# First phase of a fused decoder layer: queue order, value rows and gate chunks resequenced

## The reference, cut to what matters

```
x = x + attention(layernorm(x))      # 16 heads of 32, one shared K and V head, RoPE,
                                     # K, V squeezed to 8 and grown again, then
                                     # K = quant_dequant_8bit(K), V the same: min and max over ALL sequences
                                     # windows of 128 tokens every 64, sigmoid scores / their sum, blended
x = x + wkv(w, u, layernorm(x), ctx) # a decaying scan over tokens
x = x + ffn(layernorm(x))            # h = silu(q(x) @ tern(Wg)) * (q(x) @ tern(Wu)), rms norm, q(h) @ tern(Wd)
                                     # tern(W) = clip(round(W / mean|W|), -1, 1) * mean|W|
```

## Time and profile before

| | us |
|---|---|
| median of 3 timed runs (1096.98 to 1099.55) | 1097.28 |
| profiled execution, device time | 1100.16 |
| profiled execution, span of the trace | 1098.8 |
| busy: TensorE / VectorE / ScalarE / GpSimd | 878.8 / 844.1 / 706.2 / 435.7 |
| first scores of sequence 0 start | 102.00 |

### The profile page before, as it was taken

How to read it: one execution, slowest core, us unless ns; L and a number is a source line. 1 busy time by engine, 2 the same in 40 slices (tenths; PEclk the granted TensorE clock), 3 DMA queues, 4 the chain that set the end, 5 groups by cost and what they waited for, 6 DMA issues and landing times.

```text
span 1098.8 us, 22051 instructions
## 1 busy us (share of the span) xinstructions
PE 878.8 (80%) x8388; PEld 516.9 (47%) x8388; DVE 844.1 (77%) x1630; ACT 706.2 (64%) x1179; POOL 435.7 (40%) x494
## 2 busy tenths in 40 slices
PE   5883656678888888888888888989898888886665
PEld 2342545445454555555545555555455555553222
DVE  4744477887888888888887888888877888876953
ACT  0114737276868686868777777777786868684633
POOL 2100113236263635353535453535454444444522
PEclk9986776869999999999999999999999999997878
DMA  8876424020515151515142524242424343212022
GB/s 328 314 231 246 151 100 148 19 85 10 103 59 103 55 107 54 107 51 99 63 95 67 84 78 84 78 84 79 84 78 72 91 67 95 68 59 40 28 59 67
DMA packets 125754, 106.90 MB, mean 97 GB/s; under 512 B 99312, under 2 KB 101088, under 8 KB 124496
## 3 DMA queue, kind: packets, MB, share of 16 engines
q1 hardware_dynamic: 119344, 101.47, 35.6%
q0 software_dynamic: 624, 2.59, 0.7%
q10 hardware_dynamic: 5680, 1.42, 0.6%
HBM read 65.62 MB, written 10.49 MB: 69 GB/s over the span
## 4 chain that ended last, share of the span: by engine, by line
ACT 30%; PE 26%; DVE 20%; issue 15%; SPq 5%; DMA 2%; POOL 2%; DVEq 0%; ACTq 0%; POOLq 0%
PE bank L508 9%; ACT arena L734 6%; PE bank L607 5%; PE bank L527 4%; ACT L786 3%; ACT sums L741 3%; DVE junk L1160 3%; PE bank L597 3%; ACT sums L746 2%; ACT junk L786 2%; ACT junk L791 2%; DVE amax L1126 2%; DVE fs L1169 2%; ACT L757 2%; ACT L734 2%
## 5 line engine op out<-in xcount | busy, mean ns | idle before, releaser
L597 PE MATMUL bank<-w_up_gate,qT 128*128 128x512 bf16 x1024 | 244.9, 389 | 40.4 <-ACT junk L786 20.6
L1364 POOL TENSOR_TENSOR work<-junk,lnw 128x512 f32<-128x512 f32 x128 | 188.3, 1491 | 126.0 <-DVE junk L1160 111.7
L1347 POOL TENSOR_TENSOR sums<-sums,blend 128x448 f32<-128x448 f32 x64 | 73.6, 1170 | 274.2 <-ACT sums L746 274.2
L597 PEld LDWEIGHTS bank<-w_up_gate,qT 128*128 128x128 bf16 x1024 | 97.2, 100 | 155.8 <-ACT junk L786 26.3
L508 PE MATMUL bank<-wide,wq_sb 128*128 128x256 f32 x512 | 120.8, 397 | 34.8 <-DVE rows L1061 30.8
L607 PE MATMUL bank<-w_down,work 128*128 128x512 bf16 x512 | 132.0, 408 | 19.8 <-ACT junk L786 10.5
L508 PEld LDWEIGHTS bank<-wide,wq_sb 128*128 128x128 f32 x512 | 100.6, 199 | 61.2 <-issue 46.9
L734 ACT ACTIVATE arena<-bank 128x384 f32<-128x384 f32 x256 | 104.9, 497 | 36.0 <-PE bank L527 35.8
L527 PE MATMUL bank<-wide,k_win 32*128 32x128 f32 x1536 | 69.7, 317 | 72.9 <-ACT arena L734 54.2
L786 ACT ACTIVATE junk<-bank,deq 128x512 f32<-128x512 f32 x128 | 86.3, 686 | 54.0 <-PE bank L597 52.2
L559 PE MATMUL bank<-wo_sb,wide 128*128 128x512 f32 x256 | 115.8, 607 | 2.6 <-DVE wide L1054 2.6
(11 more groups left out here) (150 smaller groups left out, 1536.9 us busy)
## 6 DMA issues: line engine op xcount, KB each, us to landing
sums<-in_xT SPq DMA_DIRECT2D x8, 1024.0 KB, 11.2
wide<-in_xT SPq DMA_DIRECT2D x16, 512.0 KB, 3.8
rows<-in_x SPq DMA_DIRECT2D x16, 512.0 KB, 4.9
ctx_T<-in_ctxT SPq DMA_DIRECT2D x16, 512.0 KB, 3.7
wide<-wide SPq DMA_DIRECT2D x64, 128.0 KB, 2.0
out<-rows SPq DMA_DIRECT2D x32, 256.0 KB, 2.1
kv_b<-k_raw SPq DMA_DIRECT2D x16, 384.0 KB
work<-in_wgT SPq DMA_DIRECT2D x4, 1024.0 KB, 16.4
```

What stands on the lines that cost most here:

```text
L597: last = te.matmul(bank[4 + k % 4][:, :], qT[:, c, t * P:(t + 1) * P], w_up_gate[:, m, c, cols], start=c == 0, stop=c == NC - 1)
L1364: ge.tensor_tensor(hid_w[:, t, cols], hid[:, n % 2, :], lnw[:, cols], op=ALU.mult).then_inc(z_set.sem, 1)
```

## The change

On SyncE: `wkvT` and `low_rank` lead the queue, in place of ScalarE's; `wkvT` is laid out so that each partition reads one piece of 1536 B. In each pair the columns come before the rows. The wait for the small weights goes. `wq` and `xT` of sequence 0 are issued within pair 5. Gate chunks 2 and 3 are issued after the swaps of sequence 0.

```
+        sy.dma_start(wkv_sb.rearrange("p c n -> p (c n)"), a["wkvT"]).then_inc(first_loads.sem, 16)
+        sy.dma_start(low_rank, a["low_rank"]).then_inc(first_loads.sem, 16)
         for j in range(PAIRS):
+            load_columns(j)
             load_x(j)
-            load_columns(j)
-            if j == 0:
-                sy.wait_ge(first_loads.sem, first_loads.at(0))
             if j >= 3:
                 store_trig(j - 3)
-        sy.dma_start(wq_sb[:, :, :], ...)
-        load_queries(0)
+            if j == 5:
+                sy.dma_start(wq_sb[:, :, :], ...)
+                load_queries(0)
         load_keys(0)
         load_weights(GATE, 0)
+        store_trig(5)
         load_weights(GATE, 1)
-        store_trig(5)
-        load_weights(GATE, 2)
-        load_weights(GATE, 3)
         store_trig(6)
...
                 turn_queries(b, 1)
+            if i == 0:
+                load_weights(GATE, 2)
+            if i == 0:
+                load_weights(GATE, 3)
```

```
             se.copy(raw[j % 4], grown).then_inc(key_raw.sem, 1)
-            se.dma_start(v_scratch[2 * j:2 * j + 2].rearrange("u (t p) e -> p (u t) e", p=P), v_raw[j % 4])...
+            new = bank[TOK_BANK[j % 2]][:, 0:4 * 2 * HD].rearrange("p (u t g e) -> p g u t e", u=2, t=NT, g=2)[:, 1]
+            se.copy(v_rows[j % 4][:, :, 0:NW:2, :], new).then_inc(val_rows.sem, 1)
+            se.copy(v_rows[j % 4][0:BLK, :, 1, :], new[BLK:P, :, 0, :]).then_inc(val_rows.sem, 1)
+            se.copy(v_rows[j % 4][BLK:P, :, 1, :], new[0:BLK, :, 1, :]).then_inc(val_rows.sem, 1)
+            se.wait_ge(val_rows.sem, val_rows.at(j))
+            se.dma_start(v_scratch[j], v_rows[j % 4])...
...
-            windows = bass.AP(v_scratch.tensor, v_scratch[b].offset, [[HD, P], [BLK * HD, NW], [1, HD]])
-            sy.dma_start(v_q, windows).then_inc(kv_loaded.sem, 16)
+            sy.dma_start(v_q, v_scratch[pair, :, b % 2]).then_inc(kv_loaded.sem, 16)
```

More of the change, by code:

```diff
@@ L158, in build @@
     raw = [small(P, 2 * 2 * NT * HD).rearrange("p (g n e) -> p g n e", g=2, n=2 * NT) for k in range(4)]
-    v_raw = [raw[k][:, 1] for k in range(4)]
+    v_rows = [home[:, n * 2 * NW * HD:(n + 1) * 2 * NW * HD].rearrange("p (u k e) -> p u k e", u=2, k=NW) for home in
+              (q_tok[:, :, :].rearrange("p t d -> p (t d)").bitcast(fp32), qT[:, :, :].rearrange("p c s -> p (c s)").bitcast(fp32))
+              for n in both]
     wkv_sb = small(P, NC * 3 * HD).rearrange("p (c n) -> p c n", c=NC)
@@ L212, in build @@
     key_grown, key_raw, key_ext = event("key_grown", 2), event("key_raw", 2), event("key_ext", 2)
+    val_rows = event("val_rows", 3)
     w_summed, w_round, w_bound, w_tern = [
@@ L462, in keys_grow @@
                 te.wait_ge(key_raw.sem, key_raw.at(j - 1))
+            if j >= 2:
+                te.wait_ge(val_rows.sem, val_rows.at(j - 2))
             te.matmul(bank[6][0:HD, :], grown_by[:, 0:HD], roped.rearrange("p u s -> p (u s)"), start=True,
@@ L494, in tensor_program @@
                 keys_grow(j - 1)
-            if j == PAIRS - 1:
+            if j == PAIRS - 2:
                 te.wait_ge(wq_loaded.sem, wq_loaded.at(0))
@@ L502, in queries @@
                 te.wait_ge(wq_centred.sem, wq_centred.at(0))
-                te.wait_ge(key_raw.sem, key_raw.at(PAIRS - 2))
+                te.wait_ge(val_rows.sem, val_rows.at(PAIRS - 2))
             if b:
@@ L670, in scalar_program @@
     def scalar_program(se):
-        se.dma_start(wkv_sb, a["wkvT"].rearrange("(c p) n -> p c n", p=P)).then_inc(first_loads.sem, 16)
-        se.dma_start(low_rank, a["low_rank"]).then_inc(first_loads.sem, 16)
         for dst, src in ((ident[:, :], "ident"), (rope_kv, "rope_kv")):
@@ L795, in scalar_program @@
         sum_weights(GATE, 1)
-        sum_weights(GATE, 2)
         for i in range(B + 3):
@@ L818, in scalar_program @@
                 probs(b, 0)
+            if i == 0:
+                sum_weights(GATE, 2)
             if do_f:
@@ L822, in scalar_program @@
                 probs(b, 1)
+            if i == 0:
+                sum_weights(GATE, 3)
+            if do_b:
                 probs(b, 2)
@@ L1000, in vector_program @@
                 keys_rope(j)
+            if j == PAIRS - 1:
+                queries_centre()
             if j:
@@ L1282, in vector_program @@
                 round_weights(DOWN, 3)
-            if i == 0:
-                round_weights(GATE, 1)
             if do_w:
@@ L1292, in vector_program @@
                 round_weights(UP, 1)
+            if i == 0:
+                weight_mean(GATE)
+            if i == 0:
+                round_weights(GATE, 0)
+            if i == 0:
+                round_weights(GATE, 1)
             if do_f:
@@ L1484 @@
         "wqT": g["L0_attn_wq"].reshape(H, HD, D)[:, PAIRED].reshape(D, D).T, "woT": g["L0_attn_wo"].T,
-        "wkvT": np.concatenate([wk[PAIRED], wk[PAIRED], g["L0_attn_wv"]]).T,
+        "wkvT": np.concatenate([wk[PAIRED], wk[PAIRED], g["L0_attn_wv"]]).T.reshape(NC, P, 3 * HD).transpose(
+            1, 0, 2).reshape(P, NC * 3 * HD),
         "low_rank": np.concatenate([squeeze.T, grow_k, grow_v], 1),
@@ L1497 @@
     k_scratch = nc.dram_tensor("k_raw", (B, HD, 3 * S), fp32).ap()
-    v_scratch = nc.dram_tensor("v_raw", (B, S, HD), fp32).ap()
+    v_scratch = nc.dram_tensor("v_raw", (B // 2, P, 2, NW, HD), fp32).ap()
     build(nc, a, out, k_scratch, v_scratch)
```

14 lines of the change are left out of this document (2 added, 12 removed).

## The result

| | before | changed |
|---|---|---|
| median of 9 runs, us | 1096.98 (1094.6 to 1099.66) | 1101.66 (1099.52 to 1105.44) |
| profiled execution: device time, span | 1100.16, 1098.8 | 1100.92, 1099.6 |
| scores of sequence 0 start | 102.00 | 91.80 |
| up chunk 0 issued | 105.60 | 106.82 |
| `probs(0, 3)` ends | 116.79 | 117.79 |

The account below looks back on a forecast made before the run. It took two overloaded DMA engines to bound the front: savings of 11.4 us put scores at 90.6, but the gate sums return most, leaving 1.8 us gained: 1097.28 - 1.8 = 1095.4 us, range 1089 to 1100.

Parts of the forecast that it names:

- The lanes: Front, before scores: two of sixteen DMA engines overloaded by trig stores hold SyncE's queue; 128 KB cost 3.4 to 3.5 us.
- The sum for the swap: Sequence 0's swaps: four savings, 2.2 + 5.1 + 1.4 + 2.7 = 11.4 us, scores start at 90.6.
- small weights: Head of SyncE's queue: loading `wkvT` and `low_rank` first closes an early DMA gap, worth 2.2 us (1.6 to 2.5).
- the swaps: SyncE's queue: swaps ahead of gate chunks 2 and 3 save 5.1 us, and 1.4 from `wo` and `lnw` coming later.
- the values: Scratch stores and load of value rows: larger pieces save 2.7 us, 1 for the load and 0.2 per store.
- the early `wq`: `wq` and `xT` of sequence 0 in pair 5: queries at about 71.6, not 78.88; worth 0 alone, enabling other savings.
- The hole near 11 us: DMA engines, 10.2 to 12.7 us: share 0.37 because SyncE waits for `wkvT`; the change closes this gap.
- The gate chain: Gate sums between probabilities, then mean, scale and rounding: done at 105.4, so up chunk 0's issue doesn't move.
- The landing of up chunk 0: Up load: lands at 111.4, with 1.0 us of `wo` and `lnw` in front (bounds 0 and 5.1).
- B: Slower rival, chance 0.14: ScalarE's wait for the up load ahead of `probs(0, 3)` loses 5 us, 1102.3.
- A: Faster rival, chance 0.35: DMA lanes relieved more than allowed, scores at 86.9, gain 5.5 us, 1091.8.
- C: Same-time case, chance 0.51: gain 3.3 to loss 3, including a fixed later wait at up reduction and rounding, 1097.3.

Follow-up runs that it names:

- Swaps only: Kernel before, with gate chunks 2 and 3 loaded behind the swaps of sequence 0 and summed and rounded in the changed kernel's order: ratio 1.0063.
- `wo` earlier: Changed kernel, with GpSimd issuing the loads of `wo` and `lnw` ahead of the gate reduction: ratio 1.0013 to the kernel before.
- up 0 summed later: Changed kernel, with the sum of up chunk 0 moved behind `probs(0, 3)` and the logs, just ahead of chunk 1's: ratio 1.0043 to the kernel before.
- up sums behind: Changed kernel, with the sums of up chunks 0 and 1 both behind the logs and inverses of groups 2 and 3: ratio 0.9975 to the kernel before.
- even lanes: Changed kernel with gate chunks back in their old place, trig stores and K loads split, `wo` and `lnw` ahead of the gate reduction: 1081.87 us, 0.9846 to before.
- front only: Changed kernel, with gate chunks 2 and 3 loaded, summed and rounded where the kernel before has them: ratio 0.9964 to the kernel before.

## Why the prediction was wrong, step by step

**The lanes, right.** The trig stores bound the front: cutting them alone moved the scores by 18 us. That the slow engines are two is read from the share of 0.13; the trace gives the mean of the sixteen engines and not each one's work.

**The sum for the swap, right in size.** Forecast 11.4 us, measured 10.2 (scores at 91.80 for 90.6). Its parts: small weights 2.0 for 2.2; the front as a whole 4.7 for 4.9 (2.2 + 2.7); the swaps 7.2 for 6.5 (5.1 + 1.4). Within the front, the values and the early `wq` weren't tried apart, so no run shows the 2.7 us of the value rows. Queries came at 75.36 and not near 72, without effect: the rotation still waited 5.40 us for its swap.

**The hole near 11 us, right, with one name wrong.** SyncE is held by `wkvT` and `low_rank` together. `low_rank`, issued at 1.24 us, lands last, 10.0 us later, and SyncE goes on at 11.24; `wkvT` had landed at 10.5. The change moves both, so the sum stands. The prediction's reading of the late landing takes each piece of 384 B for a packet of its own. The Trainium skill ("DMA: Bandwidth & Descriptors", Queues, rings and completion order) says that an engine drains a whole packet, typically 9 to 17 descriptors, before it switches. So the reading needs more than the page states, and no run here shows it: the change moved the queue and the piece size together.

**The gate chain, right, 1.4 us short.** The issue of up chunk 0 was forecast at 105.4 and came at 106.82, 1.2 us later than before with scores 10 us sooner. "Swaps only" shows the same without the new front: scores 7.2 us sooner, issue 4.2 us later.

**The landing of up chunk 0: a mis-sized term.** I put 1.0 us of `wo` and `lnw` in front of it, with bounds of 0 and 5.1. The load took 7.4 us from issue, where it had taken 5.0: the term is 2.4 us and not 1.0. With the issue 1.4 us late that makes 114.27 for 111.4.

**The step that failed:** "Behind it `dens`, `nums`, the blend and `attention_out` follow `probs(0, 3)`, and the up matrix's sums follow on ScalarE: both move by the same 1.8 us." The sums follow their loads as well, and the load of up chunk 1 was not priced. It stands on SyncE's queue behind up chunk 0, the K load and 512 KB of `xT`, so it doesn't follow ScalarE. The forecast needs its sum at 121.88 - 1.8 = 120.08. But before, it landed at 121.2, 15.6 us after the issue of up chunk 0. With the forecast's own issue at 105.4 that gives 121.0, so even without any delay by `wo` and `lnw` the gain could be 0.9 us at most, and not 1.8.

In the changed kernel it landed at 125.6. The loss of 3.98 us at the residual adds up at this load: 1.2 us because up chunk 0 is issued later, 3.2 us because up chunk 1 lands 18.8 us after that issue in place of 15.6, less the 0.7 us that it had in hand before; the rest is 0.2. The 3.2 us go with `wo` and `lnw`. In all kernels with the K load in one piece, up chunk 1 lands 15.4 to 16.8 us after the issue of up chunk 0 where GpSimd issued its pair 10.6 us ahead of it or more, and 18.1 to 19.8 where it issued them 4.5 to 5.4 us ahead. "`wo` earlier" takes them out of the way. It has the forecast's end of `probs(0, 3)`, and is still 1.4 us slower than before by the ratio, not 1.8 faster. By the ratios the whole miss is 5.3 + 1.8 = 7.1 us, and 3.8 of it go with `wo` and `lnw`. Each ratio has an interval of 1.2 to 1.9 us to either side, so such a split is rough.

**The rivals.** B had the direction and the cause (`wo` and `lnw` in front of the up load, and all that now stands between scores and the sum), with a chance of 0.14. Its place was wrong: with `probs(0, 3)` 10.8 us sooner nothing is gained, as "up 0 summed later" shows. At its own place it came to 1.0 us (117.79 for 116.79). A and its condition did not occur: the scores came later than forecast. C, the forecast's own case, reached to a loss of 3; the loss was 4.7. But C named what holds the residual, the up matrix's reduction and rounding, and took them as fixed: they follow the last of the up loads and sums, and came 4.0 us later. (1097.28 - 1.8 is 1095.5 and not 1095.4; nothing hangs on it.)

**What stays open.** The whole front gave 4.7 us and the small weights alone 2.0; the 2.7 us left are what I had put down to the values, but the early `wq` and `xT` changed with them and weren't tried apart. The chain from the sum of up chunk 1 to the residual is read step by step in both kernels; that GpSimd's total starts 3.7 and 3.8 us after the reduction in them and 0.29 us in "up sums behind" has no cause that the rows show. That up chunk 1 lands 15.6 us after the issue of up chunk 0 with `wo` and `lnw` long gone is in part the K load: cut in four, it is 11.6 us in "even lanes". The order behind the swaps costs 9.2 us on slow lanes (1.0048 less 0.9964) and 9.4 on even ones. Its start is known, the later issue of the up matrix, but not whether another placing of the loads behind it would win it back.

## What to carry to other kernels

When work is resequenced, follow the chain past the wait that you moved to the next instruction that waits for a transfer, and then to the one after that: here the first was priced and the second, which had only 0.7 us in hand, decided. How much a load has in hand can be read before the change is made: its issue plus its time to landing, against the start of what uses it. Where a swap gives 10 us to one consumer by pushing another's input back, the question is which of them the rest stands behind, and one experiment that frees the first (here the sum of up chunk 0 moved away) answers it. And here a DMA share of 0.13 in a profile was worth more than any order of the queue: 16 us for cutting the stores whose outermost dimension is 2, against 4.0 us for "front only", the better half of this change.

## What the runs showed of the hardware

The trig stores are 1 MB in all, sixteen transfers of 64 KB. Cutting each into two took 16 us (1.5%) off the kernel. The bytes and rows are the same; with the stores whose outermost dimension is 2 there are stretches with a share of 0.13, the share of two of sixteen engines, and with the broadcast load whose outermost dimension is 4 one of 0.24, that of four of sixteen. Once cut, the first have a share of 1.06 (41 to 43 us), and the tail of the second, five microseconds with shares of 0.51 to 0.19, is down to about one. Loads that SyncE had issued behind such a transfer landed late although the engines' mean share was low: with the trig stores cut the scores came 18 us sooner, and with the K load cut up chunk 1 landed 14.0 us after the issue of up chunk 0, where it took 18.8.

The Trainium skill ("DMA: Bandwidth & Descriptors", Rules for kernel authors) says that the count of engines follows the slowest dimension that isn't 1, and that an outermost dimension below 16 confines the whole transfer to at most so many engines. By that rule the traces agree: 0.13 x 16 = 2.1 and 0.24 x 16 = 3.8.
